# A hand-written order of calls on four engines, chosen anew, in a one-core vision tower

## The chip, the cores and the metric

The kernel runs on one core of a Trainium2 chip, as one program on five instruction queues: TensorE (PE), VectorE (DVE), ScalarE (ACT), GpSimd (POOL) and the DMA queue of SyncE (SP). The metric is the device time of one execution in microseconds, the median over the runs.

## The reference

For 64 images, 196 tokens each, width D = 256, all in float32:

```python
h = patchify(x) @ tok_W.T + tok_b                          # 768 -> 256
z = layernorm(h)
xn = z / max(norm(z) * D**-0.5, eps) * g
uv = silu(xn @ uv_w.T)                                     # u 512, v 512, base 128
q, k = rope(base * gamma + beta)                           # two sets of gamma, beta
kernel = square(relu((q @ k.T + w_rel[idx]) / sqrt(128)))  # per image, 196 x 196
h = h + z * res_scale + (u * (kernel @ v)) @ o_w.T
y = layernorm(h)
logits = y @ W_in.T + b_in                                 # 8 trees of 255 nodes, depth 7
# from the root, each tree follows logits > 0 to one leaf; only visited nodes count
h = h + (silu(logits) * visited) @ W_out.T
```

## The kernel before

**Tiling.** A unit is two images, 392 tokens, so there are 32 units. Activations lie with the features on the partitions and the 392 tokens along the free axis. Nearly every product is made of float32 values split into a high and a low part: a `product` is three matmuls (lines 1168 to 1170), and each needs its operand as a high part, written by ACT (`high`, line 551), and a low part, raw minus high, written by DVE (`low`, line 861). Both inputs of `low` lie in SBUF where the raw value does (`x_low`, `hid_low`, `v_low`, `mix_low`, `kern_low`); where it lies in PSUM (`xn_low`, `ffn_x_low`) only one does.

**Stages of a unit.** `embed` (six calls, each two products into `hid_ps`), `copy_h` (ACT moves the result to `hT`), `turn_h` (eight transposes to token-major), `norm_stats` and `norm_moments` (DVE; four `bn_stats`, then a chain of operations on 98x4 elements, lines 891 to 911), `norm_roots` (POOL; a power, then one or two small products), `norm_apply` (ACT, four), `make_xn`, `turn_xn`, `turn_normed`, then base, v, u, scores, mix and `project_o`, `update_h`, and the second norm by the same steps (`turn_h(.., 1, ..)`, `norm_stats(.., 1, ..)`, `norm_roots(.., 1)`, `norm_apply(.., 1, ..)`, `turn_ffn_x`). Then eight trees: `tree_logits`, `decisions` (DVE), `tree_visits` (one bf16 matmul of 392 columns), `silu_tree`, `mask` (DVE), `hid_high`, `hid_low`, `tree_out` into `out_acc`.

**Leaves of trees 0 to 3.** Their last level isn't computed as a product. `find_leaf` (PE, four matmuls of one column) and `leaf_number` (ACT) give a row number for each token; `fetch_rows` (POOL, four indirect DMAs a tree) gathers the rows; `leaf_dots` (DVE, four operations of 98x257 elements with both inputs in SBUF) gives logits; `leaf_silu` and `scale_rows` (ACT, four) scale the rows; `sum_rows` (POOL, line 496, 98x1024 elements) adds them up; `add_rows` (PE) adds the sum to `out_acc`.

**Order.** Each engine runs its own list of calls, `body(p, i, n, nx)`, written out by hand. In a turn of the loop, unit `n` is in its first part, `i` a unit earlier, `p` two earlier, and `nx` is the next to load; the loop runs 28 times, with bodies before and after it in which some of the four are `None` and their calls do nothing. Every call waits on semaphores for what it needs and for the buffer that it overwrites, so an engine's list is the only thing that orders it. Some waits that matter here: `norm_apply(n, 1, 0)` waits for all sixteen leaf dots of the unit before (it overwrites their operand `leaf_x`); `sum_rows(i, s)` waits for `scale_rows(i, s)`; `tree_visits(i, 0)` waits for `decisions(i, 0)`; `find_leaf(i, 0)` for `mask(i, 0)`; `turn_h(n, 0, 0)` for both `copy_h`; `x_high(n, k)` for the embed call three earlier. On POOL, `late_splits` are the splits of late weights, done in the first turns only.

Of the kernel before, what the change touches and what calls it, by code (L numbers as in the profile page):

```python
# [117 lines left out]
def vit_tower(nc, x, cols, tok_w, uv_w, o_w, in_w, out_w, rel, rope, anc, ident_in, out):  # L118
    ctx = ExitStack()
    with ctx:  # L120
# [152 lines left out]
        def first(n):  # L273
            return isinstance(n, int) and n == 0
# [164 lines left out]
        def _(pool):  # L439
# [66 lines left out]
            def body(p, i, n, nx):  # L506
                late_splits(i, n, 0)
# [4 lines left out]
                fetch_rows(i, 0, 1)  # L512
                fetch_rows(i, 0, 3)
                fetch_rows(i, 0, 2)
                fetch_rows(i, 1, 0, n)
                fetch_rows(i, 1, 1)
                late_splits(i, n, 3)
                fetch_rows(i, 1, 3)
                fetch_rows(i, 1, 2)
                fetch_rows(i, 2, 0)  # L520
                fetch_rows(i, 2, 3)
                fetch_rows(i, 2, 1)
                fetch_rows(i, 2, 2)
                late_splits(i, n, 4)
                sum_rows(i, 1)
                fetch_rows(i, 3, 0)
                fetch_rows(i, 3, 2)
                fetch_rows(i, 3, 1)
                fetch_rows(i, 3, 3)
                norm_roots(n, 1)  # L530
                sum_rows(i, 2)
                norm_roots(nx, 0)
# [16 lines left out]
        def _(act):  # L549
# [206 lines left out]
            def body(p, i, n, nx):  # L756
                silu_tree(p, 7, 1)
                ffn_x_high(i, 0)
                ffn_x_high(i, 1)
                silu_tree(p, 7, 0)  # L760
# [4 lines left out]
                silu_tree(i, 0, 0)  # L765
                norm_apply(n, 0, 0)
                silu_tree(i, 1, 0)
                leaf_number(i, 0)
                norm_apply(n, 0, 1)
                make_xn(n, 0)  # L770
                hid_high(i, 0)
                norm_apply(n, 0, 2)
                make_xn(n, 1)
                norm_apply(n, 0, 3)
                make_xn(n, 2)
                silu_tree(i, 2, 0)
                make_xn(n, 3)
                xn_high(n, 0)
                hid_high(i, 1)
                xn_high(n, 1)  # L780
                silu_tree(i, 3, 0)
                x_high(nx, 0)
                leaf_number(i, 1)
                silu_base(n)
                silu_v(n, 0)
                hid_high(i, 2)
                scale_base(n, 1)
                v_high(n, 0)
                leaf_number(i, 2)
                silu_v(n, 1)  # L790
                leaf_silu(i, 0)
                scale_base(n, 0)
                hid_high(i, 3)
                v_high(n, 1)
                silu_v(n, 2)
                silu_tree(i, 4, 1)
                x_high(nx, 1)
                v_high(n, 2)
                qk_high(n, 0)
                qk_high(n, 1)  # L800
                silu_tree(i, 4, 0)
                leaf_number(i, 3)
                silu_u(n, 0)
                silu_v(n, 3)
                scale_rows(i, 0)
                x_high(nx, 2)
                silu_u(n, 1)
                silu_tree(i, 5, 1)
                kern_high(n, 0)
                v_high(n, 3)  # L810
                hid_high(i, 4)
                kern_high(n, 1)
                silu_u(n, 2)
                silu_u(n, 3)
                leaf_silu(i, 1)
                if first(n):
                    build_rows()
                silu_tree(i, 5, 0)
                scale_rows(i, 1)
                silu_tree(i, 6, 1)  # L820
                mix_high(n, 0)
                mix_high(n, 1)
                mix_high(n, 2)
                mix_high(n, 3)
                silu_tree(i, 6, 0)
# [12 lines left out]
                hid_high(i, 6)  # L838

# [19 lines left out]
        def _(dve):  # L859
# [216 lines left out]
            def body(p, i, n, nx):  # L1076
                norm_stats(n, 0, 0)
                norm_stats(n, 0, 1)
                norm_moments(n, 0)
                decisions(i, 0)  # L1080
                hid_low(p, 7)
                mask(i, 0)
                decisions(i, 1)
                hid_low(i, 0)
                decisions(i, 2)
                mask(i, 1)
                final(p)
                decisions(i, 3)
                xn_low(n, 0)
                hid_low(i, 1)  # L1090
                xn_low(n, 1)
                residual(n, 0)
                residual(n, 1)
                if first(n):
                    build_toward()
                x_low(nx, 0)
                mask(i, 2)
                leaf_dots(i, 0)
                mask(i, 3)
                hid_low(i, 2)  # L1100
                rotate_qk(n, 1)
                v_low(n, 0)
                decisions(i, 4)
                rotate_qk(n, 0)
                hid_low(i, 3)
                v_low(n, 1)
                qk_low(n, 0)
                qk_low(n, 1)
                v_low(n, 2)
                decisions(i, 5)  # L1110
                mask(i, 4)
                add_rel_bias(n, 0)
                square_relu(n, 0)
                leaf_dots(i, 1)
                add_rel_bias(n, 1)
                decisions(i, 6)
                square_relu(n, 1)
                kern_low(n, 0)
                v_low(n, 3)
                kern_low(n, 1)  # L1120
                x_low(nx, 1)
                hid_low(i, 4)
                gate(n, 0)
                mask(i, 5)
# [5 lines left out]
                gate(n, 3)  # L1130
                mix_low(n, 3)
                leaf_dots(i, 2)
# [12 lines left out]
                x_low(nx, 5)  # L1145
                hid_low(i, 6)
                ffn_x_low(n, 0)
                ffn_x_low(n, 1)
                mask(i, 7)
# [15 lines left out]
        def _(pe):  # L1165
# [253 lines left out]
            def body(p, i, n, nx):  # L1419
                make_u(i, 0)  # L1420
                tree_visits(p, 4)
                tree_logits(p, 5, 1)
                scores(i, 0)
                make_u(i, 1)
                tree_logits(p, 6, 0)
                scores(i, 1)
                tree_visits(p, 5)
                make_u(i, 2)
                tree_logits(p, 6, 1)
                make_u(i, 3)  # L1430
                tree_out(p, 3, 0)
# [3 lines left out]
                mix(i, 3)  # L1435
                tree_visits(p, 6)
                tree_out(p, 3, 1)
                tree_logits(p, 7, 0)
                project_o(i, 0, range(0, 3))
                project_o(i, 0, range(3, EC))  # L1440
                project_o(i, 1, range(0, EC))
                embed(n, 0)
# [23 lines left out]
                if first(n):  # L1466
                    turn_rows()
                tree_visits(i, 1)
                tree_out(p, 6, 1)
                tree_logits(i, 3, 0)  # L1470
                add_rows(p)
                tree_out(p, 7, 0)
                tree_out(p, 7, 1)
                turn_xn(n, 0)
                turn_xn(n, 1)
                tree_logits(i, 4, 0)
                find_leaf(i, 1)
                tree_out(i, 0, 0)
                tree_out(i, 0, 1)
                turn_normed(n, 0)  # L1480
                tree_visits(i, 2)
                tree_out(i, 1, 0)
                turn_normed(n, 1)
                make_base(n)
                make_v(n, 0)
                tree_visits(i, 3)
                tree_out(i, 1, 1)
                find_leaf(i, 2)
                make_v(n, 1)
                make_v(n, 2)  # L1490
                tree_logits(i, 4, 1)
                find_leaf(i, 3)
                tree_out(i, 2, 0)
                tree_logits(i, 5, 0)
                make_v(n, 3)
                tree_out(i, 2, 1)
# [92 lines left out]
```

## Time and profile before

| what | value |
|---|---|
| median of 3 runs | 2025.92 us (2025.3 to 2026.82) |
| the profiled execution's own time | 2028.2 us |
| its span, first to last instruction | 2026.4 us |
| mean granted TensorE clock | 0.991 |
| busy share of the span | PE 97%, weight loads 92%, DVE 84%, ACT 69%, POOL 49% |
| DMA | 163 MB, 80 GB/s over the span |

In the page's 40 slices PE is at nine tenths from the third slice to the last but one. Matmuls are pipelined: one of 392 columns is shown as 0.34 us long though the next begins 0.18 us after it, so a wait of less than 0.16 us doesn't show as idle time of PE. It has to be read from the starts.

### The profile page before, as it was taken

The numbers are of one execution on the slowest core, as the hardware profiler recorded it, in microseconds if no ns is written. First come the engines' busy times: TensorE is split into PE (matmuls) and PEld (weight loads), VectorE is DVE, ScalarE is ACT, GpSimd is POOL, SyncE is SP. The second block draws the span as 40 slices with busy tenths as digits, with TensorE's granted clock in tenths as the row PEclk, the third lists the DMA queues.
The fourth block names the chain that finished last, engine by engine and source line by source line (L and its number), as shares of the span: only waits on it lengthen the run. The fifth ranks groups of instructions, "written<-read, shape, count | busy, mean of one in ns | idle before, by whom it ended". The sixth has DMA issues, their size and how long they took to land. (4 is left out here: it accounts for less than half of the span.)

```text
span 2026.4 us, 41146 instructions
## 1 busy us (share of the span) xinstructions
PE 1973.2 (97%) x12488; PEld 1858.1 (92%) x12488; DVE 1702.8 (84%) x4210; ACT 1397.2 (69%) x3085; POOL 1001.6 (49%) x1001
## 2 busy tenths in 40 slices
PE   6799999999999999999999999999999999999997
PEld 5689999999999999999999999999999999999986
DVE  5598888898888898888898888898888898888875
ACT  5467776677776676776676776676776776776764
POOL 2675445545445545445545545545545545545544
PEclk8999999999999999999999999999999999999999
DMA  4423223223222223223233223232223233222222
GB/s 131 108 75 93 76 77 82 79 72 90 77 75 81 78 76 87 74 77 80 75 83 84 75 76 82 73 86 83 75 75 81 74 87 83 75 75 79 61 68 80
DMA packets 81999, 163.12 MB, mean 80 GB/s; under 512 B 17102, under 2 KB 48048, under 8 KB 81968
## 3 DMA queue, kind: packets, MB, share of 16 engines
q0 software_dynamic: 40960, 103.02, 19.3%
q1 hardware_dynamic: 41008, 59.71, 10.3%
q8 instruction: 16, 0.26, 0.1%
q14 instruction: 15, 0.12, 0.0%
HBM read 148.76 MB, written 13.90 MB: 80 GB/s over the span
## 5 line engine op out<-in xcount | busy, mean ns | idle before, releaser
L483 POOL DMA_INDIRECT leaf_rows<-leaf_table,leaf_at x512 | 582.2, 1137 | 156.0 <-issue 156.0
L861 DVE TENSOR_TENSOR hid_lo<-hid,hid_hi 128x392 fp32r<-128x392 f32 (+1 forms) x256 | 255.3, 997 | 77.3 <-ACT hid_hi L551 77.2
L1168 PE MATMUL out_acc<-hid_hi,outw_lo 128*128 128x392 f32 x768 | 300.3, 391 | 0.2 <-DVE hid_lo L861 0.2
L456 POOL TENSOR_TENSOR inv_root<-to_root,minus_half 98x8 f32<-98x8 f32 x64 | 95.7, 1495 | 412.7 <-DVE to_root L911 266.1
L1168 PE MATMUL hid_ps<-ffn_x,in_lo 128*128 128x392 f32 x768 | 272.1, 354 | 1.8 <-ACT hid L706 0.7
L1170 PE MATMUL out_acc<-hid_hi,outw_hi 128*128 128x392 f32 x768 | 263.4, 343 | 0.0
L1169 PE MATMUL hid_ps<-ffn_x,in_hi 128*128 128x392 f32 x768 | 262.8, 342 | 0.0
L1169 PE MATMUL out_acc<-hid_lo,outw_hi 128*128 128x392 f32 x768 | 262.2, 341 | 0.0
L1170 PE MATMUL hid_ps<-ffn_x,in_hi 128*128 128x392 f32 x768 | 261.4, 340 | 0.0
L496 POOL TENSOR_TENSOR row_sum<-leaf_rows,row_sum 98x1024 f32<-98x1024 f32 x96 | 221.3, 2305 | 40.3 <-ACT leaf_rows L743 34.6
L482 POOL TENSOR_TENSOR held<-minus_half 98x1 f32<-98x1 f32 x128 | 35.7, 279 | 373.6 <-ACT v_full L637 199.6
L1041 DVE CUSTOM_DVE_ANT_0 leaf_rows<-leaf_rows,leaf_x 98x257 f32<-98x257 f32 x512 | 195.0, 435 | 12.6 <-DMA leaf_rows<-leaf_table,leaf_at 12.6
L1022 DVE SCALAR_TENSOR_TENSOR hid<-hid_ps,hid 128x392 f32<-128x392 f32 x384 | 203.3, 557 | 0.2 <-PE hid_ps L1363 0.2
L551 ACT ACTIVATE x_hi<-x_raw 128x392 fp32r<-128x392 f32 x192 | 101.8, 530 | 144.8 <-PE hid_ps L1170 139.7
L706 ACT ACTIVATE hid<-hid_ps,col 128x392 f32<-128x392 f32 x256 | 150.0, 586 | 72.2 <-DVE decide L1006 59.1
L551 ACT ACTIVATE hid_hi<-hid 128x392 fp32r<-128x392 f32 (+1 forms) x256 | 177.0, 691 | 30.5 <-PE out_acc L1170 26.4
L1006 DVE TENSOR_SCALAR decide<-hid_ps,col 128x392 bf16<-128x392 f32 x256 | 158.5, 619 | 5.5 <-PE hid_ps L1170 4.5
L743 ACT ACTIVATE leaf_rows<-leaf_rows,leaf_act 98x256 f32<-98x256 f32 x384 | 163.0, 501 | 0.1
L1168 PEld LDWEIGHTS out_acc<-hid_hi,outw_lo 128*128 128x128 f32 x768 | 147.7, 192 | 2.7 <-issue 0.4
L1168 PEld LDWEIGHTS hid_ps<-ffn_x,in_lo 128*128 128x128 f32 x768 | 145.3, 189 | 5.1 <-issue 2.3
L1169 PEld LDWEIGHTS out_acc<-hid_lo,outw_hi 128*128 128x128 f32 x768 | 146.3, 190 | 1.5
L1169 PEld LDWEIGHTS hid_ps<-ffn_x,in_hi 128*128 128x128 f32 x768 | 145.1, 189 | 1.3
(142 smaller groups left out, 5854.6 us busy)
## 6 DMA issues: line engine op xcount, KB each, us to landing
x_raw<-x SPq DMA_DIRECT2D x192, 196.0 KB, 2.4
out<-out_stage SPq DMA_DIRECT2D x32, 392.0 KB
leaf_rows<-leaf_table,leaf_at POOLq DMA_INDIRECT x512
leaf_table<-leaf_rows SPq DMA_DIRECT2D x4, 256.5 KB, 4.2
out_stage<-in_w SPq DMA_DIRECT2D x4, 256.0 KB
tok_major<-tok_w SPq DMA_DIRECT2D x3, 256.0 KB, 4.3
late_raw<-out_w SPq DMA_DIRECT2D x6, 128.0 KB
u<-uv_w SPq DMA_DIRECT2D x1, 576.0 KB, 4.2
```

Source lines behind the costliest of these rows:

```text
L483: pool.indirect_dma_start(row_slot(s, g), None, table, bass.IndirectOffsetOnAxis(ap=leaf_at[:, s, g:g + 1], axis=0), element_offset=s * P ...
L496: pool.tensor_tensor(row_sum[:, :, :], leaf_rows[0:HALF, at:at + GROUPS, ROW_IN:ROW], row_sum[:, :, :], ALU.add).then_inc(rows_summed, 1)
L551: act.activation(out, src, ACT.Copy).then_inc(done, 1)
L706: act.activation(hid_t[:, t % 2, b], hid_ps[:, t % 2, b, 0:T], ACT.Silu, bias=bias).then_inc(activated, 1)
L743: act.activation(row_sum[:, g] if s == 0 else w, w, ACT.Copy, scale=leaf_act[:, s, g:g + 1]).then_inc(rows_scaled, 1)
L861: dve.tensor_tensor(out, src, hi.bitcast(F32), ALU.subtract).then_inc(done, 1)
L1006: dve.tensor_scalar(decide[:, t % 2], hid_ps[:, t % 2, 0, 0:T], c(COL_B_IN + 2 * t), 0.0, ALU.add, ALU.is_gt).then_inc(decided, 1)
L1022: dve.scalar_tensor_tensor(hid_t[:, t % 2, b], hid_ps[:, t % 2, 1, 0:T], VISITED[b], hid_t[:, t % 2, b], ALU.is_ge, ALU.mult).then_inc(mas ...
L1041: dve.tensor_tensor_reduce(w, w, normed2[:, g], 1.0, 0.0, ALU.mult, ALU.add, leaf_logit[:, s, g:g + 1]).then_inc(dotted, 1)
L1168: pe.matmul(out, w[1], x_parts[0], start=start, stop=False)
L1169: pe.matmul(out, w[0], x_parts[1], start=False, stop=False)
L1170: return pe.matmul(out, w[0], x_parts[0], start=False, stop=stop)
```

## The change

The lists of the four engines are put in another order. No call is added or removed, and no operation, wait, buffer or semaphore differs. Calls may also lie in the turn before or after the one they were in: `fetch_rows(.., 3, ..)`, `norm_roots(.., 1)` and `sum_rows(.., 2)` on POOL, `ffn_x_low` on DVE, and the tail of PE's list from `turn_xn` on now stand at the top of the next turn's list, under the name that the unit has there. Cut to what matters below (the lists stand as they run round, and PE's only in the stretch from `embed(n, 0)` on):

```diff
 # POOL
             def body(p, i, n, nx):
+                fetch_rows(p, 3, 0)
...
+                norm_roots(i, 1)
+                sum_rows(p, 2)
+                sum_rows(p, 3)
                 late_splits(i, n, 0)
+                norm_roots(n, 0)
                 late_splits(i, n, 1)
-                sum_rows(p, 3)
+                late_splits(i, n, 2)
                 fetch_rows(i, 0, 0)
-                late_splits(i, n, 2)
...
-                norm_roots(n, 1)
-                sum_rows(i, 2)
-                norm_roots(nx, 0)
 # DVE
+                ffn_x_low(i, 0)
+                ffn_x_low(i, 1)
                 norm_stats(n, 0, 0)
                 norm_stats(n, 0, 1)
                 norm_moments(n, 0)
                 decisions(i, 0)
+                decisions(i, 1)
                 hid_low(p, 7)
                 mask(i, 0)
...
-                decisions(i, 7)
+                hid_low(i, 5)
                 x_low(nx, 2)
                 norm_stats(n, 1, 0)
                 norm_stats(n, 1, 1)
+                x_low(nx, 3)
                 norm_moments(n, 1)
-                x_low(nx, 3)
+                x_low(nx, 4)
+                decisions(i, 7)
+                x_low(nx, 5)
                 leaf_dots(i, 3)
-                x_low(nx, 4)
-                hid_low(i, 5)
-                x_low(nx, 5)
+                mask(i, 7)
                 hid_low(i, 6)
 # ACT
+                leaf_silu(p, 3)
...
                 keep_h(i)
-                leaf_silu(i, 2)
+                x_high(nx, 2)
+                hid_high(i, 5)
                 x_high(nx, 3)
-                scale_rows(i, 2)
-                hid_high(i, 5)
                 x_high(nx, 4)
                 x_high(nx, 5)
-                leaf_silu(i, 3)
+                scale_rows(i, 2)
+                silu_tree(i, 7, 1)
+                silu_tree(i, 7, 0)
                 norm_apply(n, 1, 0)
 # PE
                 embed(n, 0)
                 turn_h(i, 1, 0)
                 turn_h(i, 1, 1)
+                embed(n, 1)
+                embed(n, 2)
                 tree_logits(p, 7, 1)
-                embed(n, 1)
-                tree_out(p, 4, 0)
-                embed(n, 2)
-                tree_out(p, 4, 1)
                 embed(n, 3)
                 embed(n, 4)
+                tree_out(p, 4, 0)
+                tree_visits(p, 7)
+                tree_out(p, 4, 1)
+                embed(n, 5)
                 turn_ffn_x(i, 0)
                 turn_ffn_x(i, 1)
-                embed(n, 5)
-                tree_visits(p, 7)
                 tree_out(p, 5, 0)
+                tree_out(p, 5, 1)
                 turn_h(n, 0, 0)
                 turn_h(n, 0, 1)
-                tree_out(p, 5, 1)
                 tree_logits(i, 0, 0)
+                tree_out(p, 6, 0)
                 tree_logits(i, 1, 0)
+                tree_out(p, 6, 1)
                 tree_visits(i, 0)
-                tree_out(p, 6, 0)
+                add_rows(p)
+                tree_visits(i, 1)
...
                 tree_logits(i, 2, 0)
                 find_leaf(i, 0)
```

In the old lists `find_leaf(i, 0)` is followed at once by `tree_visits(i, 1)`; in the new one `tree_out(p, 7, 0)` follows it. The middle of the lists (v, u, scores, mix, trees 2 to 6) is shuffled in the same manner.

## Rows read from the trace of the kernel before

**Rows 1.** Timeline of PE: `add_rows`, first unit and last but one (start us, length us, engine, line).
```profile
154.41 0.84 PE L1403 MATMUL out_acc<-ident,row_sum 98*128 98x98 f32 x8
...
1982.61 0.84 PE L1403 MATMUL out_acc<-ident,row_sum 98*128 98x98 f32 x8
```
**Rows 2.** Timeline of PE in one turn, where starts lie apart.
```profile
1242.52 0.34 PE L1169 MATMUL out_acc<-hid_lo,outw_hi 128*128 128x392 f32 x1
1242.70 0.34 PE L1170 MATMUL out_acc<-hid_hi,outw_hi 128*128 128x392 f32 x1
1243.03 1.08 PE L1203 MATMUL front<-ident,hT 128*98 128x128 f32 x8
...
1246.97 0.34 PE L1170 MATMUL hid_ps<-ffn_x,in_hi 128*128 128x392 f32 x1
1247.29 0.34 PE L1363 MATMUL hid_ps<-decide,toward 128*128 128x392 bf16 x1
...
1249.61 0.30 PE L1392 MATMUL hid_ps<-leaf_steps,taken 128*98 128x1 bf16 x4
...
1250.12 0.34 PE L1169 MATMUL out_acc<-hid_lo,outw_hi 128*128 128x392 f32 x1
...
1256.71 0.30 PE L1392 MATMUL hid_ps<-leaf_steps,taken 128*98 128x1 bf16 x4
...
1257.13 0.34 PE L1169 MATMUL out_acc<-hid_lo,outw_hi 128*128 128x392 f32 x1
```
**Rows 3.** Timeline of DVE, first norm and tree 0; brackets: idle before, and its releaser.
```profile
1243.71 1.43 DVE L878 BATCH_NORM_STATS2 stats<-front 98x6 f32<-98x256 f32 x4 [0.67 <-PE front L1203]
...
1246.61 0.63 DVE L1006 TENSOR_SCALAR decide<-hid_ps,col 128x392 bf16<-128x392 f32 x1
...
1248.51 0.56 DVE L1022 SCALAR_TENSOR_TENSOR hid<-hid_ps,hid 128x392 f32<-128x392 f32 x1
```
**Rows 4.** Timeline of DVE, second norm of the turn, the leaf dots and what follows.
```profile
1293.09 1.43 DVE L878 BATCH_NORM_STATS2 stats<-front 98x6 f32<-98x256 f32 x4
...
1295.75 0.42 DVE L1041 CUSTOM_DVE_ANT_0 leaf_rows<-leaf_rows,leaf_x 98x257 f32<-98x257 f32 x1
...
1297.14 0.56 DVE L861 TENSOR_TENSOR x_lo<-x_raw,x_hi 128x392 fp32r<-128x392 f32 x1
1297.62 2.98 DVE L861 TENSOR_TENSOR hid_lo<-hid,hid_hi 128x784 fp32r<-128x784 f32 x1
```
**Rows 5.** Timeline of POOL at the same place.
```profile
1297.23 2.54 POOL L496 TENSOR_TENSOR row_sum<-leaf_rows,row_sum 98x1024 f32<-98x1024 f32 x1
```
**Rows 6.** Timeline of POOL in the first two turns: late weights, and a sum.
```profile
61.79 0.75 POOL L448 TENSOR_TENSOR in_lo<-late_raw,in_hi 128x256 fp32r<-128x256 f32 x1
...
136.73 2.21 POOL L496 TENSOR_TENSOR row_sum<-leaf_rows,row_sum 98x1024 f32<-98x1024 f32 x1
```
**Rows 7.** Timeline of DVE at those two places.
```profile
62.14 0.42 DVE L891 TENSOR_TENSOR moments<-stats 98x4 f32<-98x4 f32 x1
...
136.75 2.48 DVE L1041 CUSTOM_DVE_ANT_0 leaf_rows<-leaf_rows,leaf_x 98x257 f32<-98x257 f32 x1 [0.81 <-DMA leaf_rows<-leaf_table,leaf_at]
```
**Rows 8.** Timeline of ACT: `scale_rows` (x4), `x_high`, second `norm_apply` (x4), `copy_h` (x2).
```profile
1293.09 1.70 ACT L743 ACTIVATE leaf_rows<-leaf_rows,leaf_act 98x256 f32<-98x256 f32 x4
...
1297.78 0.53 ACT L551 ACTIVATE x_hi<-x_raw 128x392 fp32r<-128x392 f32 x1 [1.59 <-PE hid_ps L1170]
...
1298.32 1.92 ACT L590 ACTIVATE leaf_x<-front,shift,inv_root 98x256 f32<-98x256 f32 x4
...
1302.84 1.07 ACT L574 ACTIVATE hT<-hid_ps,col 128x392 f32<-128x392 f32 x2
```
**Rows 9.** Timeline of POOL at the start: first roots, and the last split of two pieces.
```profile
21.41 1.68 POOL L456 TENSOR_TENSOR inv_root<-to_root,minus_half 98x8 f32<-98x8 f32 x1 [20.57 <-DVE to_root L911]
...
26.05 1.27 POOL L448 TENSOR_TENSOR o_lo<-late_raw,o_hi 128x512 fp32r<-128x512 f32 x1
```
**Rows 10.** Timeline of PE near the end: the last unit's `tree_visits(.., 7)`.
```profile
2013.80 0.48 PE L1363 MATMUL hid_ps<-decide,toward 128*128 128x392 bf16 x1 [8.51 <-ACT hid L706]
```

More of the change, by code:

```diff
@@ L838, in body @@
                 hid_high(i, 6)
+                ffn_x_high(n, 0)
             def uv_high(ns):
@@ L1080, in body @@
                 decisions(i, 0)
+                decisions(i, 1)
                 hid_low(p, 7)
                 mask(i, 0)
-                decisions(i, 1)
-                hid_low(i, 0)
+                x_low(nx, 0)
                 decisions(i, 2)
                 mask(i, 1)
+                hid_low(i, 0)
                 final(p)
+                hid_low(i, 1)
                 decisions(i, 3)
                 xn_low(n, 0)
-                hid_low(i, 1)
                 xn_low(n, 1)
@@ L1093, in body @@
                 residual(n, 1)
+                mask(i, 2)
+                decisions(i, 4)
+                leaf_dots(i, 0)
                 if first(n):
                     build_toward()
-                x_low(nx, 0)
-                mask(i, 2)
-                leaf_dots(i, 0)
                 mask(i, 3)
-                hid_low(i, 2)
                 rotate_qk(n, 1)
                 v_low(n, 0)
-                decisions(i, 4)
                 rotate_qk(n, 0)
-                hid_low(i, 3)
[L1106 to L1110, printed above, removed]
+                v_low(n, 1)
+                v_low(n, 2)
+                qk_low(n, 0)
+                hid_low(i, 2)
+                qk_low(n, 1)
+                decisions(i, 5)
+                v_low(n, 3)
+                add_rel_bias(n, 0)
+                hid_low(i, 3)
+                add_rel_bias(n, 1)
                 mask(i, 4)
-                add_rel_bias(n, 0)
                 square_relu(n, 0)
+                square_relu(n, 1)
                 leaf_dots(i, 1)
-                add_rel_bias(n, 1)
+                kern_low(n, 0)
+                kern_low(n, 1)
                 decisions(i, 6)
[L1117 to L1121, printed above, removed]
                 hid_low(i, 4)
                 gate(n, 0)
-                mask(i, 5)
                 gate(n, 1)
@@ L1130, in body @@
                 gate(n, 3)
+                mask(i, 5)
                 mix_low(n, 3)
+                x_low(nx, 1)
                 leaf_dots(i, 2)
@@ L1139, in body @@
                 norm_stats(n, 1, 1)
+                x_low(nx, 3)
                 norm_moments(n, 1)
-                x_low(nx, 3)
+                x_low(nx, 4)
+                decisions(i, 7)
+                x_low(nx, 5)
                 leaf_dots(i, 3)
-                x_low(nx, 4)
-                hid_low(i, 5)
-                x_low(nx, 5)
+                mask(i, 7)
                 hid_low(i, 6)
-                ffn_x_low(n, 0)
-                ffn_x_low(n, 1)
-                mask(i, 7)
             dve.sem_inc(out_stored, 16)
@@ L1419, in body @@
             def body(p, i, n, nx):
+                turn_xn(i, 0)
+                turn_xn(i, 1)
+                tree_out(p, 0, 0)
+                find_leaf(p, 1)
+                tree_logits(p, 4, 0)
+                tree_out(p, 0, 1)
+                turn_normed(i, 0)
+                tree_out(p, 1, 0)
+                turn_normed(i, 1)
+                tree_visits(p, 3)
+                make_base(i)
+                make_v(i, 0)
+                find_leaf(p, 2)
+                tree_out(p, 1, 1)
+                make_v(i, 1)
+                make_v(i, 2)
+                make_v(i, 3)
+                tree_logits(p, 4, 1)
                 make_u(i, 0)
+                find_leaf(p, 3)
+                tree_logits(p, 5, 0)
+                make_u(i, 1)
+                scores(i, 0)
                 tree_visits(p, 4)
+                tree_out(p, 2, 0)
+                scores(i, 1)
+                tree_out(p, 2, 1)
+                make_u(i, 2)
                 tree_logits(p, 5, 1)
-                scores(i, 0)
-                make_u(i, 1)
+                make_u(i, 3)
                 tree_logits(p, 6, 0)
-                scores(i, 1)
-                tree_visits(p, 5)
-                make_u(i, 2)
                 tree_logits(p, 6, 1)
-                make_u(i, 3)
-                tree_out(p, 3, 0)
                 mix(i, 0)
@@ L1435, in body @@
                 mix(i, 3)
+                tree_visits(p, 5)
                 tree_visits(p, 6)
+                tree_out(p, 3, 0)
                 tree_out(p, 3, 1)
-                tree_logits(p, 7, 0)
                 project_o(i, 0, range(0, 3))
@@ L1441, in body @@
                 project_o(i, 1, range(0, EC))
+                tree_logits(p, 7, 0)
                 embed(n, 0)
@@ L1444, in body @@
                 turn_h(i, 1, 1)
+                embed(n, 1)
+                embed(n, 2)
                 tree_logits(p, 7, 1)
-                embed(n, 1)
-                tree_out(p, 4, 0)
-                embed(n, 2)
-                tree_out(p, 4, 1)
                 embed(n, 3)
                 embed(n, 4)
+                tree_out(p, 4, 0)
+                tree_visits(p, 7)
+                tree_out(p, 4, 1)
+                embed(n, 5)
                 turn_ffn_x(i, 0)
                 turn_ffn_x(i, 1)
-                embed(n, 5)
-                tree_visits(p, 7)
                 tree_out(p, 5, 0)
+                tree_out(p, 5, 1)
                 turn_h(n, 0, 0)
                 turn_h(n, 0, 1)
-                tree_out(p, 5, 1)
                 tree_logits(i, 0, 0)
+                tree_out(p, 6, 0)
                 tree_logits(i, 1, 0)
+                tree_out(p, 6, 1)
                 tree_visits(i, 0)
-                tree_out(p, 6, 0)
+                add_rows(p)
+                tree_visits(i, 1)
+                if first(n):
+                    turn_rows()
                 tree_logits(i, 2, 0)
                 find_leaf(i, 0)
[L1466 to L1471, printed above, removed]
                 tree_out(p, 7, 0)
                 tree_out(p, 7, 1)
[L1474 to L1480, printed above, removed]
-                tree_visits(i, 2)
[L1482 to L1496, printed above, removed]
+                tree_visits(i, 2)
+                tree_logits(i, 3, 0)
             body(None, None, None, 0)
```

82 lines of the change are left out of this document (39 added, 43 removed).

## The prediction, made before the changed kernel was run

> **What bounds the kernel now.** I read the busy shares first, then the timeline of PE, and only then the lists of waits. PE is at 97%, but since its matmuls overlap on the page, a share near 100% says little; what counts is how far apart they start. In a product they start 0.178 us apart, and a call of two products takes six such steps, 1.07 us [rows 2]. From the first unit's `add_rows` to the last but one, 30 turns take 1982.61 - 154.41 = 1828.2 us, 60.94 us each [rows 1]. The rest of the span, 198 us, is the filling and emptying of the pipeline.
>
> A turn of PE has two places at which a start is late. Before `turn_h(n, 0, 0)` the step is 0.33 us instead of 0.178, so PE loses 0.15 us waiting for `copy_h`. Before `tree_visits(i, 0)` it is 0.32 us, 0.14 us lost, and the decision of tree 0 ended at 1247.24, 0.05 us before the visit began [rows 2, 3]. I found no third one in that turn. So PE sets the turn, only 0.29 us of 60.94 is there to be won by any order, and over 30 turns that is 8.7 us, 0.4%. What a new order can lose has no such bound: every wait that it puts in front of PE is lost in full.
>
> **What the new order removes.** In it, `tree_out(p, 5, 1)` stands ahead of `turn_h(n, 0, 0)`, and two `tree_out` calls lie between the first logits and the first visit. Both old waits would go if nothing else moved: -0.29 us a turn. It gives a little back: `find_leaf(i, 0)` no longer stands before `tree_visits(i, 1)`. The four small matmuls, the visit and one matmul took 1250.12 - 1249.61 = 0.51 us together; alone, the four small ones and one matmul took 1257.13 - 1256.71 = 0.42 us [rows 2]. Taking a visit as one step of 0.18 (it has as many columns), the pair costs 0.33 us side by side and 0.24 + 0.18 = 0.42 us apart: +0.09 us. PE's own floor is thus 60.94 - 0.29 + 0.09 = 60.74 us a turn. I followed the other waits of PE's list through the middle of the turn with the durations of this trace and found each released by at least about 0.1 us, so I add nothing there.
>
> **What the new order puts in the way: GpSimd's sums.** The trace shows that DVE operations with both inputs in SBUF stand still while POOL's elementwise operations run. A `hid_low` issued at 1297.62 took 2.98 us, to 1300.60, while the sum that began at 1297.23 ran to 1299.77; the timeline has 29 such. A leaf dot issued 0.02 us after a sum took 2.48 us instead of 0.42. Even a 98x4 operation of `norm_moments` issued during POOL's `in_lo` took 0.42 us and ended with it, at 62.55 [rows 4 to 7]. In the old order the sum of tree 2 begins 0.09 us after the last leaf dot has ended [rows 4, 5], and the sum of tree 3 runs after the first norm's roots; only `hid_low(i, 5)`, which has time to spare, is caught. In the new list both sums stand ahead of `norm_roots(n, 0)`, and they meet other work.
>
> The Trainium skill (SBUF — State Buffer, section "Who interferes with whom") says that a VectorE instruction with two SBUF inputs contends with a GpSimd instruction that reads SBUF, and that the one issued first holds the pair while the other blocks fully. The rows agree, 2.48 us against 0.42. If that page did not hold here, the two waits below would be absent and a turn would take the floor.
>
> *First wait, before `turn_ffn_x`.* Count from the start of `turn_h(i, 1, 0)`. Its eight transposes take about 0.9 us (1243.03 to 1247.15 less three calls of 1.07), and the stats start 0.68 us after it [rows 2, 3]. In the old list, stats, moments and one `x_low` take 1295.75 - 1293.09 = 2.66 us before the dots. The new one adds two `x_low` (0.48 each, 1297.14 to 1297.62) and `decisions` (0.63 long, of which 0.1 overlaps with the next as the `x_low` row does) [rows 4]. So the dots run from 0.68 + 2.66 + 1.49 = 4.83 to 6.22. Meanwhile ACT has `x_high(nx, 5)` after two embed calls, at 0.9 + 2.14 + 0.2 = 3.24 (0.2 is the signal: the stats start 0.68 us after the transposes, half of which take 0.45), needs about 0.42, and then `scale_rows(i, 2)`, 1.70: done at 5.35 [rows 8]. POOL's roots are done a little before that (in the old trace the sum follows the dots' start by 1.5 us, with the roots between them). The sum of tree 2 then starts at about 5.4, in the middle of the four dots. It holds two of them back for some 2.1 us, and the dots end at 8.35. `norm_apply(n, 1, 0)` waits for them, takes 1.92 us [rows 8], and ends at 10.3. PE reaches `turn_ffn_x` after the transposes, eight calls of 1.07 and a visit, at 9.6. It waits 0.7 us. Without the block the dots end at 6.2 and the four applications at 8.2, 1.4 us early.
>
> *Second wait, before `tree_visits(i, 0)`.* Count from the start of `copy_h(n, 0)`. Both copies end at 1.07 and `scale_rows(p, 3)` at 2.7 [rows 8]; the sum of tree 3 follows at once and runs to 4.9. `turn_h(n, 0, 0)` starts at about 1.2, its stats at 1.88, so the moments are due at 3.35. Their first operations have two SBUF inputs and wait until 4.9, for 1.55 us. From the start of the moments to the end of the decision is 1246.61 - 1245.17 + 0.63 = 2.07 us (1245.17 is the start of the stats plus 1.46) [rows 3], so the decision ends at 7.0. PE gets to the visit at 1.2 + 0.9 + 4 x 1.07 = 6.4 and waits 0.65 us with the signal. Then `find_leaf(i, 0)` comes 0.18 + 0.7 (`add_rows`, an estimate: eight transposes of 98 instead of 128 columns, 98/128 of 0.9) + 0.18 + 1.07 = 2.13 us after the visit; `mask(i, 0)` ends 2.46 - 0.63 = 1.83 us plus a second decision of 0.53, 2.36 us, after the first decision [rows 3], so PE waits another 0.2 us. The roots are late by the same 1.55 us; with two waits of PE behind them `turn_xn` just comes out even.
>
> Together 0.7 + 0.65 + 0.2 = 1.55 us, so a turn takes 60.74 + 1.55 = 62.29 us, 1.35 more than now. Over 29 turns (the first unit's turn is still filled by late weights) that is +39 us. Each wait has bounds: the first is 0 if the dots get through and 1.4 if the sum comes before all four; the second with its follower is 0 if the sum ends before the moments begin, and 1.5 if it catches them whole.
>
> **Start and end.** In the first turns `norm_roots(0, 0)` now stands behind the splits of two late pieces. It ran at 21.41 and the splits ended at 27.32, at most 27.32 - 21.41 - 1.68 = 4.2 us of them [rows 9]; the pieces also have to land first. Nothing else can proceed at that point, so +4 to +6 us. `norm_roots(1, 0)` is put behind a further piece in the same way, +2 to +4, partly given back where PE waits for leaf rows anyway. I take +6, between 0 and +10. At the end, PE's last `tree_visits(.., 7)` waited 8.51 us for an activation that stands behind the last leaf dots in ACT's list [rows 10]; in the new list it doesn't, but the last output and its mask still need those dots. I take -2, between -5 and 0.
>
> **The sum.** 2026.4 + 39 + 6 - 2 = 2069 us of span. The profiled execution lies 2.3 us above the median of the runs in its own time and 0.5 above it in its span, so I carry the difference of 43 us to the median: 2025.9 + 43 = 2069 us.
>
> **Rivals.**
> - *One of the two collisions only.* For: the first rests on 0.1 to 0.8 us in the times of ACT against DVE, and it would vanish if the last input piece landed late and `x_high(nx, 5)` with it. A turn then takes 60.74 + 0.7 to 0.85, about 61.5, +17 us over 29 turns, +4 for the ends: 2047 us.
> - *No collision costs PE anything, and the new order does what it can.* The waits of 0.29 us go: 29 x -0.2 = -6 us, and start and end add up to nothing: 2020 us, faster. Against it: the moments lie behind `turn_h`, which lies behind `copy_h`, and so does the sum; it decides if the sum ends within 0.9 us after the moments are due.
> - *The same, with the start paid for*: -6 + 4 = 2024 us, no change that can be measured.
> - *A worse one*: one more wait of PE that I took for even, such as `turn_xn` behind late roots, at 0.4 us or more a turn: 2081 us and above.
>
> **Chances.** Both collisions 0.58, one 0.16, a further wait 0.07, no collision and faster 0.11, no change 0.08. A measurement of this kernel tells 0.2% (4 us) from nothing. So faster 0.11, the same 0.08, slower 0.81. The range has to reach from near the last rivals to all bounds taken high: 2028 to 2090 us.
>
> **What would show it.** The distance of two `add_rows` goes to about 62.3 us. Steps: PE idle before `turn_ffn_x` (releaser ACT `leaf_x`) of some 0.7 us and before `tree_visits(i, 0)` (releaser DVE `decide`) of some 0.6; leaf dots of over 2 us and a `moments` operation of over 1 us in each turn; `hid_lo` of 784 columns no longer at 2.98. If the `moments` operations stay at 0.17 us, the second step is wrong; if the dots stay at 0.42, the first is. The prediction is wrong as a whole if the distance stays under 61.

## The result, and the profile after

The changed kernel takes 2059.87 us (median of 6 runs, 2057.96 to 2061.03) against 2026.64 us of the kernel before (6 runs): ratio 1.0164, 95% interval 1.0153 to 1.0175, slower by 33 us. The forecast was 2069 us, in a range of 2028 to 2090. The profiled execution, the fastest of the six, has a span of 2056.1 us, 29.7 more than before, at a mean granted clock of 0.991 as before.

The page says little: PE's busy time rose by 3 us, its share went from 97% to 96%.

```profile
span 2056.1 us, 41202 instructions
...
PE 1976.6 (96%) x12488; PEld 1859.3 (90%) x12488; DVE 1721.7 (84%) x4210; ACT 1381.6 (67%) x3085; POOL 953.2 (46%) x1001
```

The distance of two `add_rows` calls in the timeline of PE says it all. It is 1271.80 - 1209.61 = 62.19 us, and from the second unit's to the last one that ends a full turn, (1955.60 - 214.71) / 28 = 62.17 us, against 60.94 [rows 1].

```profile
214.71 0.84 PE L1403 MATMUL out_acc<-ident,row_sum 98*128 98x98 f32 x8
...
1209.61 0.84 PE L1403 MATMUL out_acc<-ident,row_sum 98*128 98x98 f32 x8
...
1271.80 0.84 PE L1403 MATMUL out_acc<-ident,row_sum 98*128 98x98 f32 x8
...
1955.60 0.84 PE L1403 MATMUL out_acc<-ident,row_sum 98*128 98x98 f32 x8
```

Where the turn grew is read from the steps between starts on PE, as in [rows 2]; a step without a wait is 0.178 us.

```profile
1262.27 0.34 PE L1170 MATMUL hid_ps<-x_hi,tok_hi 128*128 128x392 f32 x1
1263.03 0.89 PE L1210 MATMUL front<-ident,leaf_x 98*128 98x98 f32 x8 [0.43 <-ACT leaf_x L590]
...
1270.92 0.34 PE L1170 MATMUL out_acc<-hid_hi,outw_hi 128*128 128x392 f32 x1
1271.62 0.34 PE L1363 MATMUL hid_ps<-decide,toward 128*128 128x392 bf16 x1 [0.36 <-DVE decide L1006]
...
1273.54 0.34 PE L1170 MATMUL hid_ps<-ffn_x,in_hi 128*128 128x392 f32 x1
1274.07 0.31 PE L1392 MATMUL hid_ps<-leaf_steps,taken 128*98 128x1 bf16 x4 [0.20 <-DVE hid L1022]
```

Three starts are late: `turn_ffn_x` by 0.76 - 0.18 = 0.58 us, `tree_visits(i, 0)` by 0.52, `find_leaf(i, 0)` by 0.35; together 1.45 us. Of the two waits of [rows 2] the one before `turn_h(n, 0, 0)` is gone, it follows its predecessor at once; the one before `tree_visits(i, 0)` has grown from 0.14 to 0.52 us. What released the three late starts is in the timelines of the other engines. First POOL:

```profile
1258.26 2.40 POOL L496 TENSOR_TENSOR row_sum<-leaf_rows,row_sum 98x1024 f32<-98x1024 f32 x1 [0.30 <-ACT leaf_rows L743]
...
1267.45 2.20 POOL L496 TENSOR_TENSOR row_sum<-leaf_rows,row_sum 98x1024 f32<-98x1024 f32 x1 [6.79 <-ACT leaf_rows L743]
1270.98 1.65 POOL L456 TENSOR_TENSOR inv_root<-to_root,minus_half 98x8 f32<-98x8 f32 x1 [1.33 <-DVE to_root L911]
```

Then DVE, with the last leaf dot, the first operation of the moments, the first decisions and the mask that `find_leaf` waits for:

```profile
1258.52 2.42 DVE L1041 CUSTOM_DVE_ANT_0 leaf_rows<-leaf_rows,leaf_x 98x257 f32<-98x257 f32 x1
...
1268.04 1.63 DVE L891 TENSOR_TENSOR moments<-stats 98x4 f32<-98x4 f32 x1
...
1270.94 1.16 DVE L1006 TENSOR_SCALAR decide<-hid_ps,col 128x392 bf16<-128x392 f32 x2
...
1273.37 0.56 DVE L1022 SCALAR_TENSOR_TENSOR hid<-hid_ps,hid 128x392 f32<-128x392 f32 x1
```

And ACT's second `norm_apply`:

```profile
1261.05 1.93 ACT L590 ACTIVATE leaf_x<-front,shift,inv_root 98x256 f32<-98x256 f32 x4 [1.92 <-DVE leaf_logit L1041]
```

The sum of tree 2 begins at 1258.26, while the third dot runs; the fourth, issued at 1258.52, ends at 1260.94 (0.42 us is its own time). `norm_apply` starts 0.1 us later, having idled 1.92 us, and PE starts its transposes 0.05 us after it ends. The sum of tree 3 runs from 1267.45 to 1269.65, and a subtraction of 98x4 elements issued at 1268.04 ends at 1269.67. Both sums hold the work that the prediction named, the first one leaf dot instead of two. In the whole trace 31 leaf dots take over 2 us and 30 first operations of the moments over 1 us, while of the `hid_lo` of 784 columns, 29 of which were long before, one is, in the last unit. The roots, next on POOL, start at 1270.98 after POOL has idled 1.33 us waiting for DVE, so it is not the place behind the sum in POOL's own queue that makes them late.

### The profile page after: what moved, and what is told of

The parts are those of the page before. It is cut to its first block and busy times, and to the rows that moved or that the text cites. A ratio compares the mean times of both kernels' runs of the same rounds, so it can differ in the third digit from the quotient of the medians.

```text
span 2056.1 us, 41202 instructions
## 1 busy us (share of the span) xinstructions
PE 1976.6 (96%) x12488; PEld 1859.3 (90%) x12488; DVE 1721.7 (84%) x4210; ACT 1381.6 (67%) x3085; POOL 953.2 (46%) x1001
## 5 line engine op out<-in xcount | busy, mean ns | idle before, releaser
L483 POOL DMA_INDIRECT leaf_rows<-leaf_table,leaf_at x512 | 539.5, 1054 | 182.4 <-issue 182.4
L1168 PE MATMUL out_acc<-hid_hi,outw_lo 128*128 128x392 f32 x768 | 289.5, 377 | 1.3 <-DVE hid_lo L861 1.3
L1168 PE MATMUL hid_ps<-ffn_x,in_lo 128*128 128x392 f32 x768 | 278.2, 362 | 0.0
L861 DVE TENSOR_TENSOR hid_lo<-hid,hid_hi 128x392 fp32r<-128x392 f32 (+1 forms) x256 | 197.4, 771 | 91.2 <-ACT hid_hi L551 89.3
L1041 DVE CUSTOM_DVE_ANT_0 leaf_rows<-leaf_rows,leaf_x 98x257 f32<-98x257 f32 x512 | 249.8, 542 | 8.7 <-DMA leaf_rows<-leaf_table,leaf_at 8.7
L482 POOL TENSOR_TENSOR held<-minus_half 98x1 f32<-98x1 f32 x128 | 29.5, 230 | 350.8 <-ACT leaf_at L724 199.8
L1168 PE MATMUL hid_ps<-x_hi,tok_lo 128*128 128x392 f32 x384 | 135.4, 353 | 11.5 <-DVE tok_lo L861 7.4
```

Of the source, the lines that this page charges most:

```text
L483: pool.indirect_dma_start(row_slot(s, g), None, table, bass.IndirectOffsetOnAxis(ap=leaf_at[:, s, g:g + 1], axis=0), element_offset=s * P ...
L861: dve.tensor_tensor(out, src, hi.bitcast(F32), ALU.subtract).then_inc(done, 1)
L1041: dve.tensor_tensor_reduce(w, w, normed2[:, g], 1.0, 0.0, ALU.mult, ALU.add, leaf_logit[:, s, g:g + 1]).then_inc(dotted, 1)
L1168: pe.matmul(out, w[1], x_parts[0], start=start, stop=False)
```

## The experiments

Each was profiled and timed beside the kernel before (median 2025.5 to 2026.3 us in each set). A turn is the distance between two starts of the same call on PE, one turn apart, in the middle of the trace. Line numbers in the lines below are those of each run's own kernel: in runs 1 to 3 they are one higher from the sum on, in run 11 up to seven higher.

**1 to 3. The sums made short, the order left alone.**

```diff
                 at = GROUPS * s % ROW_SLOTS
+                w = 1 if s in (2,) else D        # or (3,), or (2, 3)
-                pool.tensor_tensor(row_sum[:, :, :], leaf_rows[0:HALF, at:at + GROUPS, ROW_IN:ROW], row_sum[:, :, :],
-                                   ALU.add).then_inc(rows_summed, 1)
+                pool.tensor_tensor(row_sum[:, :, 0:w], leaf_rows[0:HALF, at:at + GROUPS, ROW_IN:ROW_IN + w],
+                                   row_sum[:, :, 0:w], ALU.add).then_inc(rows_summed, 1)
```

> The changed kernel with the sum of tree 2 on GpSimd cut to one column of 256 (98x4 elements instead of 98x1024); the other 255 columns of that sum are left out. Every wait and every place in the lists stays. Theory (the sums' length blocks VectorE operations with two SBUF inputs): the leaf dots are no longer held, the 0.58 us before turn_ffn_x go in each turn, and the second wait shrinks a little since copy_h then ends ahead of its use: 0.58 to 0.7 us less in 29 turns, 2040 to 2043 us. Rival (the order itself puts scale_rows and tree 7's activations ahead of norm_apply on ScalarE, and the sum's length is no matter): the wait stays, 2058 to 2060 us.

> The changed kernel with the sum of tree 3 on GpSimd cut to one column of 256 (98x4 elements); the rest of that sum is left out. Theory: the moments of the first norm are no longer held for 1.6 us, and the waits before tree_visits(i, 0), 0.52 us, and before find_leaf(i, 0), 0.35 us, go: 0.87 us less in 29 turns, 2034 to 2036 us, with turn_ffn_x's 0.58 us as before. Rival (the moments are late because stats and copy_h are): 2058 to 2060 us.

> The changed kernel with both sums cut to one column of 256, the rest of both left out. Theory: all three waits go, and PE is left with its floor of 60.73 us a turn against 60.94 of the kernel before: 1.45 us less in 29 turns, 2015 to 2020 us, which is 0.3 to 0.5% below the kernel before. Rival (the order costs something besides the two collisions): above 2026 us.

| short | median us | ratio to before (95%) | turn us |
|---|---|---|---|
| sum of tree 2 | 2042.57 | 1.0074 (1.0057 to 1.0090) | 61.55 |
| sum of tree 3 | 2035.99 | 1.0047 (1.0030 to 1.0064) | 61.28 |
| both | 2016.83 | 0.9949 (0.9932 to 0.9965) | 60.63 |

Each of these kernels leaves out 255 of the 256 columns of the sums named. All three fell where the theory put them. In the second run, the sum takes 0.21 us and the moments' first operation, issued 0.6 us after its start, where a full sum would still run, takes 0.17 us. Timeline of POOL and then of DVE:

```profile
641.59 0.21 POOL L497 TENSOR_TENSOR row_sum<-leaf_rows,row_sum 98x4 f32<-98x4 f32 x1 [6.79 <-ACT leaf_rows L744]
```
```profile
642.17 0.17 DVE L892 TENSOR_TENSOR moments<-stats 98x4 f32<-98x4 f32 x1
```

Every wait and every place in the lists is as in the changed kernel, so the length of the two operations on POOL is the cause. The rivals, that ScalarE's order or a late `turn_h` makes the waits, are out. With both short, the order is 0.5% faster than the one before: what it was able to win on PE is there, and the collisions hide it.

**4. The dots ahead of the sum.**

```diff
                 x_low(nx, 4)
+                leaf_dots(i, 3)
                 decisions(i, 7)
                 x_low(nx, 5)
-                leaf_dots(i, 3)
```

> The changed kernel, whole, with leaf_dots(i, 3) moved on VectorE ahead of decisions(i, 7) and x_low(nx, 5). The dots then end about 1 us earlier, at 6.3 us after the first embed call, where the sum of tree 2 begins at 6.5; x_low(nx, 5) is caught in their place, which its reader can stand by about 0.4 us. Theory: as with the short sum of tree 2, 2040 to 2044 us. Rival (the order on ScalarE sets it): 2058 to 2060 us; if x_low is caught for longer than thought, a wait before embed(n, 5) appears in place of the one before turn_ffn_x.

2047.98 us, 1.0108 (1.0091 to 1.0124), 4 us above the top of the expectation; but the turn is 61.55 us, as with the short sum of tree 2, the wait before `turn_ffn_x` is gone and none stands before `embed(n, 5)`. The profiled execution took 2043.8 us, inside the expectation; why the timed ones lie up to 5 us above it stays open. The first collision can be undone by order alone.

**5. One collision put into the kernel before.**

```diff
                 sum_rows(p, 3)
+                norm_roots(n, 0)
+                late_splits(i, n, 0)
+                late_splits(i, n, 1)
                 fetch_rows(i, 0, 0)
 ...
                 sum_rows(i, 2)
-                norm_roots(nx, 0)
```

(The two `late_splits` at the head of the list move down with it.)

> The kernel before, whole, with one call moved on GpSimd: norm_roots(n, 0) behind sum_rows(p, 3) instead of ahead of it (ahead of the late splits, so the first unit's roots stay where they were). One of the two collisions alone, put into the old order. Theory: the sum now starts when scale_rows(p, 3) ends, about 0.6 us before the moments are due, and holds them for 1.6 us; tree_visits(i, 0) has no slack in the old list, so the whole 1.6 us shows in front of it in each turn: 29 x 1.6 = +46 us, 2066 to 2074 us. Rival (GpSimd's roots are late, but nothing is blocked, since the sum is over before the roots are due): no change, 2024 to 2030 us.

2073.71 us, 1.0236 (1.0219 to 1.0253), the turn 62.53 us. DVE, then PE, in its trace:

```profile
1084.67 1.77 DVE L891 TENSOR_TENSOR moments<-stats 98x4 f32<-98x4 f32 x1
```
```profile
1088.40 0.34 PE L1363 MATMUL hid_ps<-decide,toward 128*128 128x392 bf16 x1 [1.57 <-DVE decide L1006]
```

The time is inside the expectation. One call of GpSimd, moved past another of its own calls, costs 48 us, more than the whole change: the old list has no slack before this visit [rows 2, 3], so the 1.6 us by which the moments are held are paid in full.

**6. The second collision undone by an earlier sum.** On top of run 4:

```diff
 # ACT
-                leaf_silu(p, 3)
                 ffn_x_high(i, 1)
                 copy_h(n, 0)
                 copy_h(n, 1)
-                scale_rows(p, 3)
 ...
                 norm_apply(n, 1, 3)
+                leaf_silu(i, 3)
+                scale_rows(i, 3)
                 hid_high(i, 6)
```

> The changed kernel, whole, with leaf_dots(i, 3) early as in the run before, and leaf_silu(i, 3) and scale_rows(i, 3) on ScalarE moved from behind copy_h(n, 1) to behind norm_apply(n, 1, 3). The sum of tree 3 then starts about 2.7 us earlier and ends before the moments. Theory: all three waits go; ScalarE's list from scale_rows(i, 2) to copy_h is full, so 0.1 to 0.2 us may appear before turn_h(n, 0, 0): a turn of 60.7 to 60.9 us, 2016 to 2025 us. Rival (the sum catches ffn_x_low or hid_low instead and gives it all back): 2040 us or more.

2076.49 us, 1.0249 (1.0232 to 1.0266): a miss, and the rival's case, with a turn of 62.44 us. The moments are free, but the sum now meets `hid_low` of tree 6, and `ffn_x_low` stands behind that on DVE; PE idles 1.64 us before `turn_h(n, 0, 0)`, released by `ffn_x_low`. POOL, then DVE:

```profile
1082.86 2.20 POOL L496 TENSOR_TENSOR row_sum<-leaf_rows,row_sum 98x1024 f32<-98x1024 f32 x1 [2.50 <-ACT leaf_rows L743]
```
```profile
1083.47 2.42 DVE L861 TENSOR_TENSOR hid_lo<-hid,hid_hi 128x784 fp32r<-128x784 f32 x1 [1.74 <-ACT hid_hi L551]
1085.82 1.02 DVE L861 TENSOR_TENSOR ffn_x<-front,ffn_x 128x392 fp32r<-128x392 f32 x2
```

**7. The second collision undone by a later sum.** On top of run 4:

```diff
 # POOL
-                sum_rows(p, 3)
                 late_splits(i, n, 0)
                 norm_roots(n, 0)
+                sum_rows(p, 3)
 # PE
                 tree_visits(i, 0)
-                add_rows(p)
                 tree_visits(i, 1)
 ...
                 find_leaf(i, 0)
+                tree_logits(i, 3, 0)
+                add_rows(p)
                 tree_out(p, 7, 0)
                 tree_out(p, 7, 1)
                 tree_visits(i, 2)
-                tree_logits(i, 3, 0)
 # DVE: x_low(nx, 0) behind mask(i, 1)
```

> The changed kernel, whole, with leaf_dots(i, 3) early, sum_rows(p, 3) behind norm_roots(n, 0) on GpSimd, add_rows(p) on TensorE behind tree_logits(i, 3, 0) and with it ahead of tree_out(p, 7, 0), and x_low(nx, 0) on VectorE behind mask(i, 1). The sum falls on decisions and masks, which read PSUM and aren't held. Theory: all three waits go, and a turn takes 60.7 us: 2015 to 2020 us. Rival: the sum, 4.6 us after the moments, comes too late for add_rows, and a wait of 0.3 us or more stands there: 2025 us or more.

2048.35 us, 1.0113 (1.0096 to 1.0130), turn 61.54 us, as in run 4: a miss. `add_rows` starts 0.07 us after its sum has ended and doesn't wait visibly, but only because `find_leaf(i, 0)`, ahead of it, still waits 0.3 us for its mask, and `tree_out(p, 0, 0)` waits about 0.5 us for the final addition on DVE, since the last `tree_out` of the unit before now ends right ahead of it.

**8. The kernel before, with `leaf_silu(i, 3)` behind `silu_tree(p, 7, 0)`.**

```diff
 # ACT
                 silu_tree(p, 7, 0)
+                leaf_silu(p, 3)
 ...
                 x_high(nx, 5)
-                leaf_silu(i, 3)
```

> The kernel before, whole, with leaf_silu(i, 3) moved on ScalarE from ahead of norm_apply(n, 1, 0) to behind silu_tree(p, 7, 0) of the next turn. It tests where the changed kernel's shorter end comes from. Theory: the last tree_visits(.., 7) no longer waits 8.5 us for the last leaf dots, and PE does 5.8 us of tree_out under them: 3 to 5.5 us less at the end, the turns as before, 2020 to 2023 us. Rival (the end is set by fetch, dots, mask, sum alone): 2025 to 2027 us.

2026.26 us, 1.0001 (0.9991 to 1.0011): a miss, and the rival's time. The chain that ended last in its trace shows the next thing in the way:

```profile
2010.54 0.34 DVE leaf_rows L1041
2010.89 0.90 DVE hid_lo L861
...
2011.87 0.60 ACT hid L706
...
2012.60 0.49 PE hid_ps L1363
```

The activation of tree 7 waits for `hid_low` of tree 5, which stands behind the last dots on DVE.

**9. Run 6, with `hid_low` of tree 6 behind `ffn_x_low`.**

```diff
 # DVE
                 ffn_x_low(i, 1)
+                hid_low(p, 6)
 ...
                 mask(i, 7)
-                hid_low(i, 6)
```

> The run with scale_rows(i, 3) early, whole, and hid_low of tree 6 on VectorE moved behind ffn_x_low(i, 1). In that run PE stood 1.79 us before turn_h(n, 0, 0) waiting for ffn_x_low, which stood behind a hid_low that the early sum of tree 3 held. Theory: ffn_x_low reads PSUM and isn't held, hid_low is done at about the time that the stats are due, and the turn comes to 60.7 to 61.0 us: 2015 to 2026 us. Rival (ScalarE's full list, not the held hid_low, made the wait): 2060 us or more.

2021.18 us (2019.44 to 2025.18, 8 runs), 0.9982 (0.9972 to 0.9992): the whole computation, 1.9% faster than the changed kernel and, with an interval that excludes no change, faster than the kernel before by 4 us, which is about the 0.2% that I took as the limit of a measurement. The time is inside the expectation, the turn at its lower edge. The turn is 1063.30 - 1002.62 = 60.68 us, 0.26 less than before, which makes some 7 us; the stretch from the last `project_o` to the end, 72.0 us against 68.8, takes 3 of them back. Both sums still hold something that can stand it: the later one `hid_low` of tree 6, by 0.1 us, while the two `ffn_x_low` ahead of it take their usual 1.04 us beside the sum; the earlier one `x_low(nx, 5)`, POOL and then DVE:

```profile
1050.89 2.19 POOL L496 TENSOR_TENSOR row_sum<-leaf_rows,row_sum 98x1024 f32<-98x1024 f32 x1 [0.27 <-ACT leaf_rows L743]
```
```profile
1051.02 2.48 DVE L861 TENSOR_TENSOR x_lo<-x_raw,x_hi 128x392 fp32r<-128x392 f32 x1
```

**10. Run 7, with its two waits taken out by order.** `tree_logits(i, 3, 0)` ahead of `find_leaf(i, 0)`, `tree_out(p, 0, 0)` behind `tree_logits(p, 4, 0)`, and on ACT:

```diff
                 norm_apply(n, 0, 1)
-                leaf_number(i, 0)
                 norm_apply(n, 0, 2)
                 norm_apply(n, 0, 3)
+                leaf_number(i, 0)
```

> The run with sum_rows(p, 3) behind the roots, whole, with its two remaining waits taken away by order: tree_logits(i, 3, 0) ahead of find_leaf(i, 0), leaf_number(i, 0) on ScalarE behind the fourth norm_apply, and tree_out(p, 0, 0) behind tree_logits(p, 4, 0) instead of right behind turn_xn (it waited 0.5 us for the final addition on VectorE). Theory: a turn at PE's floor, 60.7 us, 2015 to 2021 us, faster than the kernel before by 0.2 to 0.5%. Rival (one wait gives way to another, as in the two runs before): 2030 us or more.

2038.89 us, 1.0065 (1.0049 to 1.0080): a miss again, and the rival's case. The turn is 61.26 us; the 0.3 us that `find_leaf(i, 0)` no longer waits now stand before `add_rows`, which starts 0.05 us after its sum has ended, and 0.25 us stand behind the second `find_leaf`.

**11. The kernel before, with the last unit's calls alone changed.**

```diff
 # DVE, unit 31 only: hid_low(31, 5) ahead of leaf_dots(31, 3)
+                end = isinstance(i, int) and i == UNITS - 1
+                if end:
+                    hid_low(i, 5)
                 leaf_dots(i, 3)
                 x_low(nx, 4)
-                hid_low(i, 5)
+                if not end:
+                    hid_low(i, 5)
 # ACT, unit 31 only: leaf_silu as in run 8
```

> The kernel before, whole, with only the last unit's calls changed: hid_low(31, 5) ahead of leaf_dots(31, 3) on VectorE, and leaf_silu(31, 3) behind silu_tree(31, 7, 0) on ScalarE. All turns of the loop stay as they are. In the run before this one the last visit still waited, by way of silu_tree for hid_low of tree 5, which stood behind the last dots. Theory: with that one ahead too, PE does its tree_out calls under the last fetch, 3 to 5.5 us less: 2020 to 2023 us. Rival: 2025 to 2027 us.

2023.44 us, 0.9989 (0.9980 to 0.9998): 2.1 us less, where 3 to 5.5 were expected. PE's 8.51 us before the last visit [rows 10] became two waits of 3.35 and 2.66 us:

```profile
2005.59 0.33 PE L1370 MATMUL hid_ps<-decide,toward 128*128 128x392 bf16 x1 [3.35 <-ACT hid L706]
2010.73 0.69 PE L1175 MATMUL out_acc<-hid_hi,outw_lo 128*128 128x392 f32 x1 [2.66 <-DVE hid_lo L864]
```

**12. The changed kernel, with `norm_roots(n, 0)` ahead of the first late splits.**

```diff
-                late_splits(i, n, 0)
                 norm_roots(n, 0)
+                late_splits(i, n, 0)
```

> The changed kernel, whole, with norm_roots(n, 0) ahead of the first group of late splits on GpSimd. It tests the term of +6 us at the start. Theory (what the changed trace suggests: the first unit is 3.6 us later, but the second unit's wait for late weights and leaf rows takes it up): 2057 to 2061 us, no change that can be measured, 0 to 2 us less. Rival (the start is paid in full elsewhere): 3.6 us or more less, 2053 to 2056 us.

2062.44 us, 1.0181 (1.0167 to 1.0195): nothing won, and 1.4 us above the top of the expectation. The first unit's roots run at 20.42 instead of 25.01 us, but PE's wait for `v_full` in the second unit, the first line (changed kernel), is 4.8 us longer, the second line (this run):

```profile
103.92 0.70 PE L1168 MATMUL front<-xn,uv_lo 128*128 128x392 f32 x1 [4.42 <-ACT v_full L637]
```
```profile
105.75 0.69 PE L1168 MATMUL front<-xn,uv_lo 128*128 128x392 f32 x1 [9.19 <-ACT v_full L637]
```

The run doesn't isolate the first unit. The edit moves the roots of the second turn too, and there the late splits, now behind roots that wait for DVE until 77.38, begin at 79.38 instead of 74.89 us; GpSimd's first fetch comes at 93.85 instead of 91.75, and with it the leaf dots, the `v_low` behind them on DVE, and `v_full`.

## Why the prediction was right, point by point

- **PE sets the turn, 0.29 us to be won, a floor of 60.74 us.** Right. With both sums short the turn is 60.63 us, with run 9's order 60.68; and 62.17 - 1.45 is 60.72. The 0.09 us for the lost neighbourhood of `find_leaf` and visit was not measured by itself.
- **GpSimd's elementwise operations hold VectorE's with two SBUF inputs.** Right for the sums and for the late splits, but too wide: the power of `norm_roots` is elementwise too and holds nothing (last section). A small slip in the rows: in the old order the sum of tree 2 starts 0.02 us after the last dot has ended, not 0.09; that dot starts at 1296.79 and takes 0.42.
- **The first wait, 0.7 us.** Right in place and cause, 0.58 us in size; shortening that sum alone took 0.63 us from the turn. Counted from the start of `turn_h(i, 1, 0)`, 1252.84, the sum came at 5.42 us, as forecast, but the dots at 4.65 instead of 4.83, so that the third had just begun and three got through where I counted two. That was a matter of 0.1 us.
- **The second wait, 0.65 us, and its follower, 0.2.** 0.52 and 0.35 us, together 0.87 against 0.85; the near equality of the sums is luck, the first was 0.13 us smaller and the second 0.15 larger. Shortening that sum took 0.90 us from the turn, and run 5 showed the same collision in the old order at 1.6 us.
- **The sum of a turn, 62.29 us.** Measured 62.17.
- **The middle of the turn costs nothing.** Right: of the starts on PE in one turn, 1147.4 to 1209.6, only the three named come late. The other long steps are those of 512-column matmuls (0.23 us), or follow a visit, transposes or one-column matmuls.
- **Start, +6 us.** This term failed; it measures -1.1 us, outside its bounds of 0 and +10. The step was that the first unit's delay is paid, and only partly given back. PE's first `turn_xn` is indeed 3.6 us later (30.56 against 26.98), but `project_o` of the second unit starts at 124.37 against 125.46, 1.1 us earlier. Run 11 has the calls of the kernel before up to its last unit, and there it starts at 124.44, so what can be said is that nothing of the delay is left. The changed kernel's trace shows why: the second unit waits for `v_full`, that for a `v_low` which stands behind leaf dots on DVE, the dots for fetched rows, and the first fetch, at 91.75, for the late splits ahead of it on GpSimd. I had named the giving back, but priced it at 2 of 8 us.
- **End, -2 us.** From the last `project_o` to the end are 2056.1 - 1992.41 = 63.7 us against 2026.4 - 1957.62 = 68.8, so -5.1, at the edge of my bound. But the two stretches had different mean granted clocks, 0.96 and 0.90. Run 12, with the calls of the changed kernel there, took 67.2 us at 0.90, which is -1.5 against the kernel before. So -2 may have been about right, and much of the rest the clock's; one pair of traces doesn't prove it. The reason given was incomplete in any case: runs 8 and 11 show that the activation alone brings nothing, and together with `hid_low(.., 5)` 2.1 us.

Between those two marks, 30 units apart, the changed kernel takes 1868.0 us against 1832.2, +35.9; with -1.1 and -5.1 that is the 29.7 us of the spans. The forecast had +39, +6 and -2, together 43: it was 13 us too high in the span, 3 in the turns, 7 at the start and 3 at the end, all to the same side. The medians lie 33 us apart, and the forecast only 9 us off, since the profiled execution of the changed kernel was 1.9 us below its median and that of the kernel before 1.6 us above.

## What to carry to other kernels

An order of calls has to be judged with what each operation excludes on other engines, not only with what it waits for: here 2.2 us on an engine that is idle half of the time was worth up to 1.6 us a turn on the busiest. Before a GpSimd call like this sum is moved, list what VectorE issues in its window, and see that each operation there with two SBUF inputs has slack of the call's length, as has what is queued behind it. When one collision is undone, the call meets other work, so look where it lands: three of the four reorderings built on run 4 met a new wait, and the fourth brought the gain.

## What the runs showed of the hardware that was not expected

The size of the held operation doesn't matter. Each stood until the sum had ended, and then took about its own time less 0.14 us: the 98x4 operation ended 0.02 us after the sum (it took 1.63 us in the changed kernel and 1.77 in run 5, instead of 0.17), the 98x257 dot 0.28 us after it, the 128x784 `hid_low` of run 6 0.83 us after it. VectorE operations that read PSUM were not held: in run 7 a decision and the two operations of a mask took 0.63, 0.56 and 0.56 us, their usual times, while the sum ran from 1200.02 to 1202.21. Where they were queued behind a held one, they were late with it.

The holding goes both ways. A sum alone takes 2.2 us; it took 2.40 when issued 0.08 us after the start of the third dot, and 2.54 in the kernel before, issued 0.09 us after the start of an `x_low` [rows 4, 5].

The power on GpSimd, 1.3 us long on 98x4 elements, held nothing. In the kernel before it runs from 1295.42 to 1296.74:

```profile
1295.42 1.32 POOL L456 TENSOR_TENSOR inv_root<-to_root,minus_half 98x4 f32<-98x4 f32 x1 [4.90 <-DVE to_root L901]
```

The leaf dots that DVE issued meanwhile, at 1295.75 [rows 4], 1296.10 and 1296.44, took their usual 0.42 us. Why the power differs from the sum is not shown; no run changed its size.
